# One batch's last stages run in two parts of two tiles each, in alternation

## The reference

```python
# text block; x_text is the block's normalized input, c_t its attention context
x = layernorm(x_text, g_norm_in, b_norm_in) * (1 + gate * scale_in) + gate * shift_in
y = s4d(x, ...)              # rfft over the tokens, times Kf, irfft, plus skip
y = y * (1.0 + mod_gate * scale_out) + mod_gate * shift_out
xt = x_text + y
h = layernorm(xt, g_ffn, b_ffn)
h = jax.nn.gelu(h @ W1 + b1, approximate=False) @ W2 + b2   # 128 -> 512 -> 128
xt = xt + h
return layernorm(xt, g_norm_out, b_norm_out)                # added to x by the caller
# quantized product, on layernorm(x)
lhs_scale = max|lhs| over the features / 127;  q_lhs = round(lhs / lhs_scale) as int8
return (q_lhs @ q_rhs) * lhs_scale * rhs_scale              # added to x by the caller
```

## Time and profile before

| | |
|---|---|
| runs | 598.66, 598.63, 603.07 us |
| profiled execution: its own time | 599.79 us |
| profiled execution: span, first to last instruction | 598.0 us |
| PE busy in the span | 467.0 us (78%) |
| DVE busy | 419.7 us (70%) |
| ACT busy | 268.4 us (45%) |
| POOL busy | 145.6 us (24%) |
| stretch from the last inverse transform to the end, 554.4 to 598.0 us | 43.6 us |
| in it PE, DVE, ACT, POOL busy | 17.18, 17.09, 4.81, 4.31 us |

### The profile page before, as it was taken

The page is one execution under the profiler, slowest core; times in us unless marked ns, Lnnn a source line. Parts: engine busy times, 40 slices in busy tenths (PEclk is TensorE's granted clock), DMA queues, the critical chain, the costliest instruction groups (busy, mean ns, idle before and its releaser), DMA issues.

```text
span 598.0 us, 8713 instructions
## 1 busy us (share of the span) xinstructions
PE 467.0 (78%) x2763; PEld 354.5 (59%) x2763; DVE 419.7 (70%) x1746; ACT 268.4 (45%) x546; POOL 145.6 (24%) x214
## 2 busy tenths in 40 slices
PE   5376063676999899999999999999999999515460
PEld 4131022465886598873897886587888887303330
DVE  3459564838277457687888798799889798995326
ACT  4245442367536456555356645537455445301020
POOL 3511265243510003003101601401231402321100
PEclk9997675588999899999999999999999999957785
DMA  8708500000210000200000200000000000000000
GB/s 177 142 8 256 151 1 1 1 1 2 39 15 4 1 1 16 40 4 1 1 2 0 54 3 2 2 19 1 1 2 2 19 0 2 0 1 19 0 1 18
DMA packets 16159, 15.02 MB, mean 25 GB/s; under 512 B 1194, under 2 KB 14258, under 8 KB 16114
## 3 DMA queue, kind: packets, MB, share of 16 engines
q1 hardware_dynamic: 16114, 14.47, 10.6%
HBM read 9.15 MB, written 1.05 MB: 17 GB/s over the span
## 4 chain that ended last, share of the span: by engine, by line
PE 65%; DVE 18%; issue 5%; ACT 5%; POOL 3%; DMA 2%; SPq 1%; POOLq 0%; DVEq 0%
PE moe_h L827 18%; PE moe_y L839 17%; PE side L782 5%; PE side L880 3%; PE side L890 3%; PE side L898 2%; PE side L868 2%; PE side L906 2%; PE side L689 2%; DVE area L1280 2%; PE side L751 1%; PE side L767 1%; PE side L854 1%; DVE TOP L1270 1%; DVE xn_head L1180 1%
## 5 line engine op out<-in xcount | busy, mean ns | idle before, releaser
L1032 ACT ACTIVATE HT<-moe_h,W 128x256 f32<-128x256 f32 x256 | 115.7, 472 | 110.4 <-PE moe_h L827 109.9
L827 PE MATMUL moe_h<-xnT_moe,W 128*128 128x256 f32 x512 | 141.4, 396 | 4.7 <-ACT HT L1032 3.8
L839 PEld LDWEIGHTS moe_y<-W,HT 128*128 128x128 f32 x1024 | 134.6, 195 | 9.8 <-issue 2.9
L839 PE MATMUL moe_y<-W,HT 128*128 128x128 f32 x1024 | 137.3, 279 | 0.0
L827 PEld LDWEIGHTS moe_h<-xnT_moe,W 128*128 128x128 f32 x512 | 89.6, 197 | 19.2 <-issue 9.0
L1256 DVE SCALAR_TENSOR_TENSOR X<-moe_y,RW,X 128x128 f32<-128x128 f32 x128 | 38.6, 343 | 24.0 <-PE moe_y L839 23.4
L782 PE MATMUL side<-PT,VP 128*72 128x512 f32 x80 | 43.5, 631 | 0.4 <-ACT PT L1012 0.4
L1280 DVE MATCH_REPLACE8 area<-TOP,area 128x77 f32<-128x77 f32 x192 | 40.5, 222 | 0.0
L1012 ACT ACTIVATE PT<-side 128x512 f32<-128x512 f32 x40 | 23.3, 594 | 17.6 <-PE side L767 14.2
L1270 DVE MAX8 TOP<-area 128x8 f32<-128x77 f32 x192 | 31.2, 224 | 0.0
L1570 POOL TENSOR_TENSOR area<-area 128x128 f32<-128x128 f32 x16 | 7.8, 490 | 90.6 <-ACT area L1055 90.6
(11 more groups left out here) (318 smaller groups left out, 834.9 us busy)
## 6 DMA issues: line engine op xcount, KB each, us to landing
W<-in_w SPq DMA_DIRECT2D x8, 512.0 KB, 8.9
QA<-Q SPq DMA_DIRECT2D x24, 128.0 KB, 3.9
X<-in_x SPq DMA_DIRECT2D x4, 256.0 KB, 6.7
out_dram<-FO SPq DMA_DIRECT2D x4, 256.0 KB, 2.3
KM<-area SPq DMA_DIRECT2D x6, 160.0 KB, 5.5
V<-in_vpack SPq DMA_DIRECT2D x1, 579.0 KB, 7.9
area<-in_r2pack SPq DMA_DIRECT2D x1, 576.0 KB, 5.8
area<-in_gpack SPq DMA_DIRECT2D x1, 576.0 KB, 8.7
```

The costliest lines, as they stand in the source:

```text
L827: pe.matmul(moe_h[n % 2][:, 0:HS], W1[:, e, c * P:(c + 1) * P], xnT_moe[:, b % 2, h * HS:(h + 1) * HS], start=True, stop=True).then_inc(mo ...
L839: mm = pe.matmul(moe_y[m % 2][:, t * P:(t + 1) * P], HT[:, m % 2, c, t * P:(t + 1) * P], W2[:, e, c, :], start=(c == 0), stop=(c == HC - 1))
L1032: act.activation(HT[:, m % 2, c, :], moe_h[n % 2][:, 0:HS], ACT.Relu, bias=wc("b1")[:, e * HC + c:e * HC + c + 1]).then_inc(moe_h_ready, 1)
```

## The change

The last batch's steps from `idft` on are written twice, for part 0 (tiles 0 and 2) and part 1 (tiles 1 and 3). Part 0 stays in stream `O`, part 1 is a new stream `Z`, and the table ends in `O6 Z O Z O Z ...`: each step of part 0 is followed by the same step of part 1, on every engine. `turn(b, i)` is the count that a semaphore has then. Rows of tiles are `part(b, i)`, a slice with step 2. Each part is stored by itself (128 KB). Batches 0 to 2 run as before, and the order of their instructions is unchanged.

```diff
+def half_steps(b, h):
+    ffn, out, quant = (k + (str(h) if b == LAST else "") for k in ("ffn", "out", "quant"))
+    return [("idft", b, h), ("s4_out", b, h), ("ln_stats", b, ffn),
+            ("ln_apply", b, ffn), ("norm_T", b, ffn), ("ffn_up", b, h), ("ffn_down", b, h),
+            ("ln_stats", b, out), ("ln_apply", b, out), ("ln_stats", b, quant), ("ln_apply", b, quant),
+            ("quant", b, h), ("quant_T", b, h), ("quant_mm", b, h)]
+
 def tail_steps(b):
+    return [("dft", b, 0), ("spectrum", b, 0)] + half_steps(b, 0)
...
+def part(b, i):
+    h = half_of(b, i)
+    if h is not None:
+        return slice(h, T, 2)
+    return slice(0, T) if i not in TEXT else slice(TEXT.index(i) * HT_, (TEXT.index(i) + 1) * HT_)
...
-E8 T E C E O C U O E8 C E3 T O E T C E3 T O E2 C E C O T U T U4 T5 O T3 O T O T2 O T5 O T3 O19
+E8 T E C E O C U O E8 C E3 T O E T C E3 T O E2 C E C O T U T U4 T5 O T3 O T O T2 O T5 O T3 O6 Z O Z O Z O Z O Z O Z
+O Z O Z O Z O Z O Z O Z O Z O Z
...
                 if kind == "quant_mm":
-                    sp.wait_ge(out_ready, b + 1)
-                    sp.dma_start(out[b].rearrange("(t p) d -> p t d", p=P), FO[:]).then_inc(out_stored, 16)
-            sp.wait_ge(out_stored, 16 * B)
+                    sp.wait_ge(out_ready, turn(b, i))
+                    r = part(b, i)
+                    sp.dma_start(out[b].rearrange("(t p) d -> p t d", p=P)[:, r], FO[:, r]).then_inc(out_stored, 16)
+            sp.wait_ge(out_stored, 16 * (B + 1))
...
                 if kind == "idft":
-                    for half in range(2):
+                    for half in range(2)[part(b, i)]:
...
-                        pe.matmul(dst[:], vc("w1f")[:, c * P:(c + 1) * P], xnT["ffn"][:], start=True, stop=True)\
+                            pe.matmul(dst[:, 0:HS], vc("w1f")[:, c * P:(c + 1) * P], xnT["ffn"][:, i * HS:(i + 1) * HS],
+                                      start=True, stop=True).then_inc(full, 1)
...
                 if kind == "ln_stats":
-                    pool.wait_ge(ln_ve[i], b + 1)
+                    k = norm_of(i)
+                    pool.wait_ge(ln_ve[k], turn(b, i))
...
                 if kind == "ffn_up":
-                    pool.tensor_tensor(X3b[:], X3b[:], rc("b2f").unsqueeze(1).broadcast_to((P, T, D)), ALU.add)\
+                    r = part(b, i)
+                    pool.tensor_tensor(X3b[:, r], X3b[:, r],
+                                       rc("b2f").unsqueeze(1).broadcast_to((P, len(tiles_of(b, i)), D)), ALU.add)\
                         .then_inc(x3b_ready, 1)
```

More of the change, by code:

```diff
@@ L180, in unit_at, with tiles_of @@
     return m // (HN * E8), (m // E8 % HN, m % E8)
[L183 to L185 removed]
+def tiles_of(b, i):
+    return range(T)[part(b, i)]
 def needed(step, former):
     kind, b, i = step
+    if kind in HALVED and half_of(b, i) == 1:
+        first = (kind, b, 0 if i == 1 else i[:-1] + "0")
+        return [first] + ([former] if former is not None else [("spectrum", b, 0)])
     if kind == "smax":
@@ L973, in _ @@
                         act.activation(xnT_moe[:, b % 2, :], src[:], ACT.Copy).then_inc(read, 1)
+                    elif half_of(b, i) is not None:
+                        h = half_of(b, i)
+                        act.activation(xnT["ffn"][:, h * HS:(h + 1) * HS], src[:, 0:HS], ACT.Identity, bias=vc("bf"),
+                                       scale=vc("gf")).then_inc(read, 1)
                     elif i == "ffn":
@@ L1065, in _ @@
                         src, read = filled(act, kind, b, i, c)
-                        act.activation(GL[:, c, :], src[:], ACT.Gelu, bias=vc("b1f")[:, c:c + 1]).then_inc(read, 1)
+                        o = slice(0, S) if b < LAST else slice(i * HS, (i + 1) * HS)
+                        act.activation(GL[:, c, o], src[:, 0:o.stop - o.start], ACT.Gelu, bias=vc("b1f")[:, c:c + 1]).then_inc(read, 1)
                 if kind == "kgen_base":
@@ new lines, in _ @@
+                    if k == "ffn":
+                        dve.wait_ge(s4_ready, n)
+                    if k == "out":
+                        emptied(dve, "ffn_down", b, half_of(b, i) or 0)
+                    if k == "quant":
+                        dve.wait_ge(x5_ready, n)
+                    for t in tiles_of(b, i):
+                        ins = dve.bn_stats(st[k][:, t, :], src[:, t, :])
+                    ins.then_inc(ln_st[k], 1)
+                    dve.wait_ge(ln_st[k], n)
+                    for t in tiles_of(b, i):
+                        ins = dve.bn_aggr(mv[k][:, t, :], st[k][:, t, :])
@@ new lines, in _ @@
+                    ins.then_inc(ln_mv[k], 1)
+                    dve.wait_ge(ln_mv[k], n)
+                    dve.tensor_scalar(ve[k][:, r], mv[k][:, r, 1], EPS, None, ALU.add).then_inc(ln_ve[k], 1)
+                if kind == "ln_apply":
+                    k = norm_of(i)
+                    n = turn(b, i)
+                    r = part(b, i)
+                    src = {"ffn": X3b[:], "out": X4[:], "quant": xnorm["out"][:]}.get(k, X[:, b])
+                    dve.wait_ge(ln_rstd[k], n)
+                    if k == "out" and b >= 1:
@@ L1376, in _ @@
+                    o = i * HS if b == LAST else 0
+                    dve.tensor_scalar(qbT[:, o:o + n], src[:, 0:n // 2].bitcast(BF16), -QMAX, None, ALU.max).then_inc(read, 1)
                 if kind == "quant_mm":
```

168 lines of the change are left out of this document (85 added, 83 removed).

## The result

The changed kernel takes 592.92 us (median of nine runs, 591.72 to 594.65) against 598.59 (median of nine, 597.28 to 603.07): a ratio of 0.9894 with a 95% interval of 0.9869 to 0.9919. That is 5.67 us, where 4.7 were forecast (594.0). The profiled execution spans 590.2 us.

A forecast was written before the change was run, and what follows sets the result against it. The prediction took the single-file order of the last 44 us as the bound, with slack on every engine. Savings of 2.77 + 1.5 + 0.4 = 4.7 us from 598.66 gave 594.0, range 592.3 to 597.0.

The forecast's parts named there:

- Up to the transposes: From the last inverse transform through additions, norm and transposes: `ffn_up` starts at 566.38 in place of 568.33, 1.95 us earlier.
- The collision: POOL's bias addition of part 0 runs beside DVE's apply 1 and stretches it: 0.44 us lost.
- The feed-forward block: `ffn_up` and `ffn_down`: clock rises 3.8 us after `ffn_up` starts; DVE starts on part 1 2.77 us earlier, first lead included.
- 570.2 on its scale: Sign on TensorE's clock in `ffn_up`: prediction wrong if the rise lies more than 2 us from 570.2.
- The vanished 0.87: PE's wait of 0.87 us before `ffn_down` is gone; part 1's Gelu is covered by half of `ffn_down` (1.9 us).
- Norms and quantization: From DVE's last `ffn_down` addition to its last instruction: 15.2 us against 16.72, 1.5 us less.
- Store: Last store moves 128 KB in place of 256 KB at the end of the span: 0.4 us less.
- clock early and no collision: Rival: apply 1 slips ahead of POOL's addition, clock rises by 568.6, `ffn_down` ends 0.95 to 1.05 earlier: 593.0; chance 0.17.
- Powers and applies do not exclude each other: Rival claimed they do: power 1 waits for apply 0 in norms "ffn" and "quant", 0.45 us each: 594.9; chance 0.10.
- Two tiles cost about half of four: Rival claimed two tiles cost as much as four, the strided view being slow: about 6 us more, 600.0; chance 0.05.
- the one in which the parts win nothing: Rival: parts go in step; only the 0.87, the 1.13s and the store are won, less added instructions: 597; chance 0.07.
- The clock did not stay low: Rival claimed the clock stays low in the feed-forward block, `ffn_up` taking 7.3 and `ffn_down` 7.6: 599.5; chance 0.06.

The follow-up runs named there:

- e10: Kernel before, unsplit, with one unread 256-column product ahead of the last transposes and one ahead of `ffn_up`: 598.52 us, ratio 0.9997.
- e13: Kernel before, unsplit, most DVE work between last inverse transform and "ffn" power left out, so `ffn_up` starts early (last batch's values wrong): one run, 597.73 us.
- e5: Changed kernel with POOL's bias addition of part 0 waiting for part 1's apply: 593.37 us, ratio 0.991 to the kernel before.
- e15: Changed kernel with three unread 256-column additions on DVE ahead of part 0's two, so the rest starts later: 595.22 us, ratio 0.9939 to the kernel before.
- e16: e13 with two unread 256-column products filling PE's pause between the last transposes and `ffn_up`: one run, 597.23 us, tail 40.89 against 42.75.
- e17: Complete kernel before with two unread 256-column products ahead of the last transposes and one ahead of `ffn_up`: 598.49 us, ratio 0.9995.
- e3: Kernel before, warmed: 8 unread products ahead of the last inverse transform and 6 ahead of the last norm's transposes: 594.5 us, ratio 0.9922.
- e4: Changed kernel, warmed: 8 unread products ahead of the last inverse transform, 5 ahead of part 0's transposes: 590.39 us, ratio 0.985 to the kernel before.
- e9: e4 plus an unread one-column Gelu behind the last forward transform's evacuation, loading Gelu's table early: 589.18 us, ratio 0.9845 to the kernel before.
- e6: Changed kernel with the two last 128 KB stores as one of 256 KB again: 592.79 us, ratio 0.9899 to the kernel before.
- e11: Split with part 0 running ahead of part 1 (skewed), plus 8 and 2 unread warming products on PE: 587.89 us, ratio 0.9818 to the kernel before.
- e12: e11 plus Gelu's table loaded early by a one-column pass: 587.96 us, ratio 0.9813 to the kernel before.

## Why the prediction was right or wrong, by its steps

**Up to the transposes: right.** Forecast 1.95 earlier, measured 1.78. The missing 0.17 is nearly all the inverse transform itself, 5.75 in place of 5.60: the first rise came 0.3 later in this trace, which other unsplit kernels show too (e10, e13). From its end to `ffn_up` it is 6.28, where 6.26 was forecast.

**The collision: right.** The addition follows power 1 without a gap, and the apply takes 1.00 (over 0.9 was forecast). e5, with the cause removed, gives 0.60, and `ffn_up` starts 0.35 to 0.38 earlier. But what it costs in the end was mis-sized: not 0.44, but under 0.2, since the rise did not move with the start and the clock took back half.

**The feed-forward block: the step that failed**, in "I place the rise as the rows have it, 3.8 us after its start". Two rows had agreed on 3.7 and 3.9, and I made a delay behind the start of the work out of them. The runs show no such delay: from `ffn_up`'s start to the rise it is 3.7 (before), 2.4 (after), 2.8 (e5), 3.9 (e10), 6.0 (e13), 4.8 (e15), 1.9 (e16), 0.2 (e17). They show two places, 14.1 to 14.5 and 17.5 to 17.9 us after the start of the inverse transform, and nothing between them in twelve traces. Which one it is depends on PE's work ahead of and in the first part of `ffn_up`, as the edits show one by one: an earlier start alone leaves it late (e13), an earlier start with the pause in front of `ffn_up` filled makes it early (e16), three products in the unsplit kernel make it early and two do not (e17, e10), and one microsecond of delay makes the split form's late (e15). That it is the filled pause which brings it forward in the split form, where part 1's transposes stand in that place, is the likeliest reading and is not shown, because no run took these transposes away at the same start. The order listed ahead of the prediction has them there, and I had used it for the start of `ffn_up` alone.

The prediction called itself wrong if the rise lay more than 2 us from 570.2 on its scale. It lay at 566.72 + 2.22 = 568.94, 1.3 off, so this sign did not show and was set too wide. In numbers: the forecast for `ffn_up` was 3.8 + 1.75 = 5.55, it took 4.80; that is 0.75 of the 0.88 us by which the tail fell below forecast. The rest is small: `ffn_down` 3.73 in place of 3.81 and starting 0.16 ahead of the modelled end of `ffn_up`, the store 0.06 better, against them the 0.17 above.

What the clock gives the change altogether is an estimate: with the rise at 17.9, `ffn_up` from 12.03 on would have had 5.9 us of low clock and ended after 6.55 (e13, from 11.89: 6.64), 1.75 later than it did. Without it the tail would have gained 3.83. So **of 5.58 us about 3.8 come from the split itself, the smaller store included, and about 1.75 from the clock**. With the clock high in both forms it is 3.87 (e3 and e4), but that this number is nearly the same is in part chance: 0.89 of table load shows in e4 and is hidden in the change, and without it the split is worth 4.76 (e3 and e9).

**The vanished 0.87: right, and its cover thin.** PE goes into `ffn_down` without a gap. I had named part 1's Gelu as hidden; the table load ahead of part 0's is hidden in the change at the low clock and not in e4 at the high one (0.71).

**Norms and quantization: right.** 15.2 forecast, 15.20 measured. Between its first and last instruction DVE is busy for 13.69 us there, in the kernel before for 12.41 of 16.72: 2.8 us of waiting were filled and 1.28 of added instructions paid for it. (The 15 added instructions of the prediction are those of the whole tail; 11 of them, 55 in place of 44, lie here.)

**Store: right,** 0.46 for 0.4, and e6 gives it back.

**The rivals.** The first, clock early and no collision, gave 593.0, and the median is 592.92. It was half right: it named the early clock, with a chance of 0.17, and the collision that it denied is there. That its time was hit so closely is partly luck, since the collision cost little for a reason that it did not have. Powers and applies do not exclude each other: power 1 at 561.94 ran beside apply 0 at 561.81, which took its 0.60 and the power 0.77 in place of 0.71. The rule of the Trainium skill (SBUF — State Buffer, "Who interferes with whom") holds here for the long addition and not for the power. Two tiles cost about half of four (0.42 against 0.69, 0.60 against 1.11), so that rival falls, and so does the one in which the parts win nothing. The clock did not stay low, though e15 shows how near a later rise is: one microsecond later, and `ffn_up` is 1.2 longer.

**The chances.** The median lay 1.06% under the kernel before, beyond my bound of 1%, for which I had given 0.14; 0.83 was on no change. The chain, the overlap and the store were priced right, and what the clock does in `ffn_up` was not; it put the size just past a bound. The spread of my forecast on its low side (593.1) was a rise 0.5 us earlier, where 1.4 was to be had.

**What stays open.** What PE must have done for the early rise is not settled: e10 had more PE work ahead of `ffn_up` than the split form and shorter pauses in it (0.22 against 0.92), and rose late. Whether e17's extra product or the filled pause made the difference was not separated. Why the first rise lies at 3.9 in some executions and at 4.2 in others, and why the start of the last inverse transform lies up to 3.5 us apart between executions, was not looked into.

## What to carry to other kernels

Splitting a serial tail into parts in alternation pays what the engines waited for each other, less the fixed part of each added instruction: here 3.8 us of 43.5, by the estimate above. Two rows that agree on a delay don't make it a rule: before a clock's rise is put into a sum as "so long after the work starts", ask what PE does ahead of that work, and price the sum at a rise one place earlier and one later. And a lock-step alternation is seldom the best order; letting part 0 run ahead was worth 4.1 us more.

## What the hardware showed that I had not expected

- Useless work made a chain shorter: four unread PE instructions in a pause of PE moved the clock's rise from 17.9 to 14.1 us and took 1.86 us off the tail (e16 against e13), some 1.5 of it not explained by the place of the first rise.
- An earlier start can be given back: starting `ffn_up` 1.92 us sooner by leaving work out gained 0.73 (e13), 1.0 us of work added cost 2.18 (e15).
- Warming the clock through the whole tail is worth 43.48 - 39.26 = 4.22 us in the unsplit form, of 598.
- A table load of 1.28 us showed in no wait of the change at the low clock, cost 0.9 us at the high one (e4, e9) and 0.2 in the skewed order (e11, e12).
- The rise behind the transposes comes 10.2 or 13.7 us after the one inside the inverse transform, and at no other place in twelve traces.
